# Sums over partitions on TensorE in four column tiles, and the 1/rms power in two halves

## The reference, cut to what matters

```python
q = rmsnorm((x @ wq.T), q_norm_w)      # per token and head: x * rsqrt(mean(x*x) + 1e-6) * w
k = rmsnorm((x @ wk.T), k_norm_w)
q, k = apply_rope(q), apply_rope(k)    # indexed by head here, so a weight per channel and head
scores = 50 * tanh((q @ k.T) * 128**-0.5 / 50)          # causal mask follows
attn = softmax(scores)                 # exp(scores), divided by its sum over keys
out = (attn @ v) @ wo.T
```

## Time and profile before

| | us |
|---|---|
| median of 3 runs | 1254.39 |
| lowest and highest | 1250.26, 1256.57 |
| the profiled execution | 1250.0 |
| its span in the profile | 1248.2 |
| mean granted PE clock, share of full | 0.977 |

### The profile page before, as it was taken

One profiled execution on the slowest core, in us unless ns is written; L12 is line 12 of the kernel. 1 busy time (PEld: TensorE's weight loads), 2 busy tenths in 40 slices (PEclk: granted clock), 3 DMA queues, 4 the chain that ended last, 5 costly groups with the idle time before them and its releaser, 6 DMA issues.

```text
span 1248.2 us, 22044 instructions
## 1 busy us (share of the span) xinstructions
PE 1134.5 (91%) x6879; PEld 960.5 (77%) x6879; DVE 1060.9 (85%) x1683; ACT 699.4 (56%) x1143; POOL 695.5 (56%) x663
## 2 busy tenths in 40 slices
PE   4689999999999999999999999999998786699998
PEld 3578888888888888888888888888887652377788
DVE  5599999999999999999999999999997869715554
ACT  3476666676667676666666666667666432022210
POOL 2466666666666666666666666666666538070011
PEclk9899999999999999999999999999999889799999
DMA  4010100000000000000010000000000160018901
GB/s 152 31 44 26 30 21 30 22 29 25 25 25 25 25 25 25 25 25 25 27 41 34 21 30 21 30 25 25 25 18 18 43 200 1 0 51 224 232 30 51
DMA packets 42143, 55.67 MB, mean 45 GB/s; under 512 B 8864, under 2 KB 34816, under 8 KB 42112
## 3 DMA queue, kind: packets, MB, share of 16 engines
q1 hardware_dynamic: 36336, 49.49, 13.2%
q10 hardware_dynamic: 5200, 4.22, 1.2%
q0 software_dynamic: 576, 1.57, 0.4%
HBM read 49.37 MB, written 4.33 MB: 43 GB/s over the span
## 4 chain that ended last, share of the span: by engine, by line
PE 35%; issue 24%; DVE 22%; POOL 11%; ACT 5%; DMA 2%; POOLq 1%; DVEq 0%; SPq 0%; ACTq 0%
PE ps L357 7%; PE ps L359 6%; PE ps L358 6%; DVE qraw L1094 5%; POOL pacc L887 5%; DVE qhat_lo L1011 5%; POOL praw L876 5%; PE ps L614 4%; PE ps L622 3%; ACT praw L710 2%; DVE qhat_hi L1021 2%; ACT prob_hi L671 2%; PE ps L639 2%; PE ps L640 2%; PE ps L563 2%
## 5 line engine op out<-in xcount | busy, mean ns | idle before, releaser
L876 POOL TENSOR_SCALAR_AFFINE_SELECT praw<-praw 128x128 f32<-128x128 f32 x256 | 164.5, 643 | 256.1 <-ACT praw L710 253.4
L671 ACT ACTIVATE prob_hi<-praw 128x1024 fp32r<-128x1024 f32 (+7 forms) x256 | 171.4, 683 | 192.2 <-POOL praw L876 189.6
L1011 DVE TENSOR_TENSOR prob_lo<-praw,prob_hi 128x1024 fp32r<-128x1024 f32 (+7 forms) x256 | 251.4, 1002 | 28.5 <-ACT prob_hi L671 27.6
L887 POOL TENSOR_TENSOR pacc<-pacc,praw 128x768 f32<-128x768 f32 (+2 forms) x192 | 236.4, 1231 | 29.5 <-POOL praw L876 27.5
L704 ACT ACTIVATE praw<-ps,rstd 128x1024 f32<-128x1024 f32 (+7 forms) x256 | 183.0, 736 | 10.3 <-PE ps L359 3.3
L357 PE MATMUL ps<-qhat_hi,kT_hi 128*128 128x512 f32 (+3 forms) x384 | 143.9, 375 | 48.8 <-DVE qhat_lo L1011 33.7
L710 ACT ACTIVATE praw<-praw 128x1024 f32<-128x1024 f32 (+7 forms) x256 | 163.5, 677 | 0.0
L864 POOL TENSOR_TENSOR rstd<-var,mhalf 128x16 f32<-128x16 f32 x32 | 125.3, 3916 | 60.0 <-DVE var L1049 60.0
L357 PE MATMUL ps<-prob_hi,vS_hi 128*128 128x512 f32 (+3 forms) x384 | 135.9, 354 | 3.0 <-DVE prob_lo L1011 3.0
L359 PE MATMUL ps<-qhat_hi,kT_lo 128*128 128x512 f32 (+3 forms) x384 | 133.5, 348 | 0.0
L358 PE MATMUL ps<-qhat_lo,kT_hi 128*128 128x512 f32 (+3 forms) x384 | 133.3, 347 | 0.0
(11 more groups left out here) (168 smaller groups left out, 2508.2 us busy)
## 6 DMA issues: line engine op xcount, KB each, us to landing
rqB<-rq_rows SPq DMA_DIRECT2D x32, 512.0 KB, 3.7
wgu<-in_wgu SPq DMA_DIRECT2D x32, 352.0 KB
wd<-in_wd SPq DMA_DIRECT2D x32, 176.0 KB
wraw<-in_wqkv SPq DMA_DIRECT2D x16, 256.0 KB, 3.7
wv<-in_wqkv SPq DMA_DIRECT2D x16, 128.0 KB, 2.1
woraw<-in_wo SPq DMA_DIRECT2D x16, 128.0 KB, 2.1
yacc<-in_x SPq DMA_DIRECT2D x1, 2048.0 KB, 14.5
x_rows<-yacc SPq DMA_DIRECT2D x2, 1024.0 KB, 8.5
```

Source lines behind the costliest of these rows:

```text
L671: return nc.scalar.activation(dst, src, ACT.Copy)
L876: nc.gpsimd.affine_select(out=diag, in_=diag, compare_op=ALU.is_ge, fill=0.0, base=0, pattern=[[1, P]], channel_multiplier=-1).then_inc(ma ...
L887: nc.gpsimd.tensor_tensor(pacc[:, b, P * j:T], before, raw, ALU.add).then_inc(pacc_done, 1)
L1011: v.tensor_tensor(dst, x_, hi.bitcast(F32), ALU.subtract).then_inc(done, 1)
```

## The change

q and k squares are no longer transposed on DVE. PE multiplies them, as moving operand, by a 128 x 32 block of ones, once per column tile g of the array: the result for tile g lands on PSUM partitions 32 g to 32 g + 31, 32 equal rows, 256 columns. For q the 256 columns are read with a step of 8 elements (32 bytes), for k and `pacc` in runs of 32. DVE transposes the PSUM bank in blocks of 32 x 32, after which one column in 32 is a token's sum. The power is done in two instructions of 8 columns, q first; SP waits for the first, the tanh for the second. Constants needed only later are made later. ACT waits with new squares until the last ones have been read.

```diff
-        ones = sb("ones", [P, 2])
+        ones = sb("ones", [P, 32])
...
+            def strip_sums(bank_no, c0, by_strip):
+
+                for g in range(BLK):
+                    last = mm(ps[32 * g:32 * g + 32, bank_no, c0:c0 + 32 * TT].rearrange("p (j r) -> p j r", r=32), ones[:, :],
+                              by_strip[:, g], start=True, stop=True, tile_position=(0, 32 * g))
+                return last
+
+            def strips(row):
+                return row.rearrange("p (j g r) -> p g j r", g=BLK, r=32)
+
             def sums_of_squares(step, count, bank_no):
 
                 open_unit(count)
-                pe.wait_ge(folded, step * 8 + 8)
-                mm(ps[:, bank_no, 0:2 * BLK * TT], fold[:, :], sqp[:, :, :, :].rearrange("p m g j -> p (m g j)"),
-                   start=True, stop=True).then_inc(pj_done, 1)
+                pe.wait_ge(qsq_done, step + 1)
+                strip_sums(bank_no, 0, qsq[:, :].rearrange("p (g r j) -> p g j r", g=BLK, r=32))
+                pe.wait_ge(ksq_done, step * 2 + 2)
+                strip_sums(bank_no, 32 * TT, strips(ksq[:, :])).then_inc(pj_done, 1)
...
-            def sums(s, b, half, count, bank_no):
-
-                if half == 0:
-                    open_unit(count)
-                    pe.wait_ge(pacc_done, (s + 1) * TT + RING)
-                for j in range(TT // 2 * half, TT // 2 * half + TT // 2):
-                    last = mm(ps[:, bank_no, j:j + 1], pacc[:, b, P * j:P * j + P], ones[:, 0:1], start=True, stop=True)
-                if half == 1:
-                    last.then_inc(pj_done, 1)
+            def sums(s, b, count, bank_no):
+
+                open_unit(count)
+                pe.wait_ge(pacc_done, (s + 1) * TT + RING)
+                strip_sums(bank_no, 0, strips(pacc[:, b, :])).then_inc(pj_done, 1)
...
                     values(s - 1, 1 - b, 7)
-                    sums(s - 1, 1 - b, 0, *hd.unit(b, "sums"))
                 scores(s, b, 2)
                 scores(s, b, 3)
                 if old:
-                    sums(s - 1, 1 - b, 1, *hd.unit(b, "sums"))
+                    sums(s - 1, 1 - b, *hd.unit(b, "sums"))
...
+            def squares_free(step):
+
+                if not (isinstance(step, int) and step == 0):
+                    act.wait_ge(folded, step)
...
                 if j == 0:
-                    act.wait_ge(r_done, s + 1)
+                    act.wait_ge(rk_done, s + 1)
...
-                nc.gpsimd.tensor_tensor(rstd[:, b, :], var[:, b, :], mhalf[:, :], ALU.pow).then_inc(r_done, 1)
+                nc.gpsimd.tensor_tensor(rstd[:, b, 0:TT], var[:, b, 0:TT], mhalf[:, 0:TT], ALU.pow).then_inc(r_done, 1)
+                nc.gpsimd.tensor_tensor(rstd[:, b, TT:2 * TT], var[:, b, TT:2 * TT], mhalf[:, 0:TT], ALU.pow).then_inc(rk_done, 1)
...
                 if what == "ss":
-                    for g in range(BLK):
-                        rows = slice(32 * g, 32 * g + 32)
-                        last = v.tensor_scalar(var[rows, b, :].rearrange("p (m j) -> p m j", m=2),
-                                               bank[rows, 0:2 * BLK * TT].rearrange("p (m g j) -> p m g j", m=2, g=BLK)[:, :, g, :],
-                                               1.0 / DH, RMS_EPS, ALU.mult, ALU.add)
-                    last.then_inc(pj_free, 1)
+                    v.transpose(sqT[:, :], bank).then_inc(folded, 1)
+                    dve.wait_ge(folded, step + 1)
+                    v.tensor_scalar(var[:, b, :], sqT[:, :].rearrange("p (n r) -> p n r", r=32)[:, :, 0],
+                                    1.0 / DH, RMS_EPS, ALU.mult, ALU.add).then_inc(pj_free, 1)
                     return
...
             def summed(b, count, bank_no):
                 dve.wait_ge(pj_done, count)
-                v.reciprocal(rsum[:, b, :], ps[:, bank_no, 0:TT]).then_inc(pj_free, 1)
+                v.transpose(sumT[:, :], ps[:, bank_no, 0:32 * TT]).then_inc(pj_free, 1)
+                dve.wait_ge(pj_free, count)
+                v.reciprocal(rsum[:, b, :], sumT[:, :].rearrange("p (j r) -> p j r", r=32)[:, :, 0]).then_inc(rsum_done, 1)
```

More of the change, by code:

```diff
@@ L511, in _ @@
                 values(s - 1, 1, j)
-            for half in range(2):
-                sums(s - 1, 1, half, *end.unit(0, "sums"))
+            sums(s - 1, 1, *end.unit(0, "sums"))
             for u in range(4):
@@ L675, in _, with projected @@
                 copy_hi(xT[0][:, :, b * T:b * T + T], xraw[:, :, b * T:b * T + T]).then_inc(xhi_done, 1)
-            def projected(what, b, count, bank_no):
+            def squares_free(step):
+                if not (isinstance(step, int) and step == 0):
+                    act.wait_ge(folded, step)
+            def projected(what, b, step, count, bank_no):
                 if what == "q":
+                    squares_free(step)
                     act.wait_ge(pj_free, count)
@@ L690, in _ @@
                 if what == "q1":
-                    projected("q", 0, n + 1, None)
+                    projected("q", 0, 0, n + 1, None)
                 elif what[0] in "kv":
-                    projected(what, 0, n + 1, PJ + n % 2)
+                    projected(what, 0, 0, n + 1, PJ + n % 2)
             def tanh(s, b, j):
@@ L848, in _ @@
             for row, col, value in ((0, 1, 1.0), (1, 1, float(P)), (2, 2, 1.0)):
-                pool.wait_ge(consts, 10 + row)
+                pool.wait_ge(consts, 6 + row)
                 nc.gpsimd.affine_select(out=rest[:, col:col + 1], in_=rest[:, col:col + 1], compare_op=ALU.not_equal, fill=value,
                                  base=-row, pattern=[[0, 1]], channel_multiplier=1).then_inc(consts, 1)
-            pool.wait_ge(consts, CONSTS - 2 * BLK)
-            nc.gpsimd.memset(fold[:, :], 0.0).then_inc(consts, 1)
-            for k in range(1 - BLK, BLK):
-                pool.wait_ge(consts, CONSTS - BLK + k)
-                nc.gpsimd.affine_select(out=fold[:, :], in_=fold[:, :], compare_op=ALU.not_equal, fill=1.0, base=-32 * k,
-                                    pattern=[[-1, P]], channel_multiplier=1).then_inc(consts, 1)
             pool.wait_ge(consts, CONSTS)
@@ L1112, in tile, with out_projected @@
                 lo_of(prob[1][:, j % RING, 0:n], praw[:, j % RING, 0:n], prob[0][:, j % RING, 0:n], plo_done)
-            def out_projected(b, u, sums_count, count, bank_no):
+            def out_projected(b, u, step, count, bank_no):
                 if u == 0:
-                    dve.wait_ge(pj_free, sums_count)
+                    dve.wait_ge(rsum_done, step + 1)
                 dve.wait_ge(pj_done, count)
@@ L1169, in step @@
                     output_lo(s - 1)
-                if new:
-                    fold_squares(s + 1, 3)
                 if old:
                     summed(1 - b, *hd.unit(b, "sums"))
-                    out_projected(1 - b, 0, hd.unit(b, "sums")[0], *hd.unit(b, "op0"))
+                    out_projected(1 - b, 0, s - 1, *hd.unit(b, "op0"))
                 if new:
@@ L1178, in step @@
                 if old:
-                    out_projected(1 - b, 1, hd.unit(b, "sums")[0], *hd.unit(b, "op1"))
+                    out_projected(1 - b, 1, s - 1, *hd.unit(b, "op1"))
                 tile(s, 1)
@@ L1240, in _ @@
             for u in range(4):
-                out_projected(1, u, end.unit(0, "sums")[0], *end.unit(0, f"op{u}"))
+                out_projected(1, u, s - 1, *end.unit(0, f"op{u}"))
             dve.wait_ge(pj_free, UNITS_ALL)
```

85 lines of the change are left out of this document (27 added, 58 removed).

## The result

The changed kernel takes 1268.06 us in the median of four runs (1264.55 to 1271.09); the kernel before took 1255.44 us beside it on the same chip (1250.26 to 1256.57). The ratio is 1.0119, with a 95% interval from 1.0093 to 1.0146: slower by 1.2%, or 12.6 us. The forecast was 1294 us and +3.2%. The side was right, the size was not.

A forecast was written before the change was run, and what follows sets the result against it. A loop of PE's work up to the sums of squares, then power, masks and DVE's list, bounds the step. Terms: -1.82 + 1.10 - 0.20 + 1.98 - 0.15 + 0.39 = +1.30 us, times 31, with ends +39: 1294 us; range 1225 to 1370.

The forecast's parts named there:

- The bound: Whole step: a loop of PE's work up to the sums of squares, then the power, masks and DVE's list.
- `var`: From the end of the sums of squares to `var`: 0.92 us instead of 1.07, a gain of 0.15.
- The split power: Power on POOL in two halves: 0.39 us more than the whole, added to the loop each step.
- early q half: q's half of the power, done some 1.7 us sooner: no gain, as its broadcast was not late.
- The strip products: Column-tile sums on PE: 1.10 us for exponentials instead of 1.82, 1.98 for squares instead of 0.20.
- Turning the array: PE switching between whole and tiled, four times a step: counted as nothing, up to 0.65 us kept for the range.
- The step of 8 on q: Rival on PE's strided q read: a record 0.31 us longer, +1.55 us a step, 1342 us; chance 0.15.
- five slots: Forecast for a group of eight records on PE: only neighbouring tiles' records overlap, 1.10 us; chance 0.36.
- DVE's relief: 5.9 us a step off DVE ahead of the sums of squares: at most 0.5 us, counted as nothing.
- the old sums on PE: Eight one-column products for the sums of exponentials removed from PE: 1.82 us off, 1.10 put in their place.
- all four at once, faster: Rival on PE: four tiles stream together, three groups in 1.32 us, -0.46 us a step, 1240 us; chance 0.22.
- The signs named: Trace signs for the forecast: starts in pairs, DVE near 22.5 us, step 31.0; wrong if a group takes under 0.7.

The follow-up runs named there:

- `before_halves`: The kernel before with only its power split into two halves of 8 columns: 1265.06 us, ratio 1.0115 to the kernel before.
- `one_power`: The changed kernel with the power in one instruction of 16 columns again: 1252.82 us, ratio 1.0002 to the kernel before.
- `k_power_late`: The changed kernel with the k half of the power moved behind the mask of tile 5 on POOL: 1218.71 us, ratio 0.9753 to the kernel before.
- `before_less_dve`: The kernel before with only the first of four fold pieces done on DVE from the second step on: 1233.3 us, ratio 0.9842.
- `sums_twice`: `one_power` with the strip products for the sums of exponentials issued twice: 1254.59 us, ratio 1.0012 to the kernel before.
- `before_k_late`: `before_halves` with the k half of the power moved behind tile 5 on POOL: 1280.97 us, ratio 1.0235 to the kernel before.
- `dve_work_back`: `one_power` with unused DVE transposes and reductions put back at the removed fold's places: 1287.12 us, ratio 1.0292 to the kernel before.

## Why the prediction was right or wrong

**The bound: right behind the sums of squares, wrong ahead of them.** The step is a loop over engines, and what lies between `var` and the masks counts nearly in full: `before_halves`, `one_power` and `k_power_late` show it three times. Ahead of the sums of squares the prediction had PE's work alone as the bound, and said that what shortens DVE there does not shorten the loop. `before_less_dve` shortened it by 0.76 us.

**The split power: right.** Forecast +0.39 us a step; measured 4.38 - 3.95 = +0.43 in the timelines, 0.48 and 0.60 in the backs of the steps. Times 31 this is the whole of the 12.6 us. That its early q half would be worth nothing also held: `rqB` was not waited for.

**The strip products: the step that failed.** They were priced at five and nine slots, 1.10 + 1.98 = 3.08 us; they took 2.05, because records start four at a time. The argument that a tile's two records keep the other tiles back, so that only the second of one and the first of the next overlap, was wrong. It rested on the rule that no record in the trace of before starts ahead of the one written before it, in a trace that had no tiled product at all, and so could not speak on that. The estimate worked out in the prediction from the Trainium skill (TensorE: Matmul & The Clock Gate, Part 3), some 1267 us, was 1 us from the measured 1268.06; part of that is chance, as it knew neither the strided q nor DVE's part.

**Turning the array: between the ends.** PE goes to the tiled products twice a step, at 0.33 - 0.23 = 0.10 us each, and back twice, at some 0.12 us. That is 0.4 us a step, within the 0 to 0.65 kept for the range. The Trainium skill (TensorEngine Tiling (Array Packing), Key Properties) says that a change of the tiling mode drains the engine; these gaps on both sides of a group, and none between q's group and k's, agree with that, though no run took another cause apart.

**The step of 8 on q: right in kind.** A q record is 0.25 us longer where the rival had 0.31; in two rounds instead of five slots this gave +0.48 us and not +1.55.

**`var`: right in price.** From the k group's last record to the power, the transpose (0.72) and the scaling (0.17) are what was forecast. But the fold product's 0.20 us became 0.90 + 0.58 = 1.48 us on the path, so from the start of the sums to the power it is 2.61 us instead of 1.53: +1.08.

**DVE's relief counted as nothing, the old sums on PE as -1.82 + 1.10: both wrong, and they hide each other.** Put right in size, PE's saving is 1.82 - 0.57 = 1.25 us. With DVE loaded none of it is seen in the way to the sums of squares (13.20 and 13.22 us, the second with 0.7 us more on DVE), with DVE relieved 0.6 us of it is (12.61 to 12.03, with 1.1 us less on DVE), and `sums_twice` shows the same from the other side (0.09 of 0.43 counts). DVE's relief was worth 0.76 us a step in the kernel before and at most 1.15 in the changed one. The idle times of DVE did not say so; that DVE finished `oT_lo` at 525.63, 0.14 us ahead of the product that reads it, did. A wait of 0.65 us behind the power was taken as a sign that DVE had slack everywhere. In the sum, a credit of 1.25 us for PE alone stood for 1.0 to 1.2 us that needs both.

**The sum again**, with the measured sizes, in one step: the way to the sums of squares -1.0, from there to the power +1.08, the power +0.43: +0.5 us, as the table has it (+0.51). In the prediction's own terms, 2.05 for 3.08 and 0.43 for 0.39 turn its +1.30 into +0.31 us a step. The 0.2 us that is missing is what is left of the terms it had at nothing: the tenths ahead of the groups, PE's wait of 0.24 us for the tanh ahead of tile 4's scores, and, the other way, DVE's relief; no run took these apart. That the result lay between "all four at once, faster" and "five slots" has the same reason: the first had the starts right, but left out the strided q (0.48) and the turning of the array (0.4).

**The signs named:** starts four within one slot, the sign named for the rival; DVE 23.2 us a step (named: near 22.5); the powers 2.58 and 1.80 us (named: 1.6 to 2.2); first mask 543.20 - 538.79 = 4.4 us behind `var` (named: 4.3); the step 30.13 us (named: 31.0); a group of 0.57 us, below the 0.7 at which the text said it would be wrong.

## What to carry to other kernels

Where a loop over engines bounds a step, splitting an operation helps only if the half that the loop doesn't need is also moved out of it: the same split was +1.2% left in place and, with its second half moved behind later masks, -2.5%. Where two engines reach the same product together, a saving on one alone shows less than its size; compare when each is ready, and test by giving the load back, not by reading idle time at one place. Before a loss is put down to an engine, look at the granted clock step by step: in `before_k_late` it split the steps into shorter and longer ones. And a price for an operation that the trace does not contain should keep both ends open: nothing in rows of whole-array products said how tiled ones start.

## What the runs showed of the hardware that had not been expected

- Four column tiles of 32 columns, float32, 256 moving columns each: eight records in 0.57 us, in two rounds of four, against 8 x 0.22 = 1.76 one by one. Sixteen take 1.00 us. Going to such products cost 0.10 us and going back 0.12.
- A moving operand read with a step of 32 bytes lengthens a float32 record from 0.39 to 0.64 us, and a round from 0.22 to 0.45 (from start to start). DVE's transpose with the same step takes 1.18 us instead of 0.70, and ACT's square of 1024 elements, written with a step of 512 bytes, 2.10 instead of 1.06. The Trainium skill (SBUF — State Buffer, Door 1, its note on cachelines) says that every access that goes to a new 16-byte line pays a penalty; the three engines agree, at 1.7 to 2.0 times.
- The power on POOL: of two equal halves back to back, the first took 2.58 us and the second 1.80, and the one that runs later beside the masks 2.62, where a quiet one took 1.64. The same instruction thus varies by 1 us within one kernel; what it goes with, no run took apart.
- Behind a DMA write of 1024 elements of 4 bytes, the read that waits for it was issued 10.6 us later, where behind 128 rows of 32 bytes it is 1.4 (541.48 to 542.89 in SP's timeline of after).
- The granted clock fell to 1.2 GHz for 3.41 us, 1.1 us behind a wait of PE of 0.91 us, in `before_k_late`, and stayed at 2.4 GHz through waits of 1.4 us in `dve_work_back`.
